# Delta-rule step: where the sums of squares and the turned values stand in the matmul queue

## The reference, cut to what matters

```
mixed_qkv = silu(causal_depthwise_conv(hidden @ Wqkv.T, conv_w))   # 4 taps
query, key, value = split(mixed_qkv)       # z, b, a: further projections of hidden
q = l2norm(query) / sqrt(128);  k = l2norm(key)
per token: state = state * exp(g);  delta = (v - k.state) * beta
           state = state + k (x) delta;  out = q.state
out = rmsnorm(out) * norm_w * silu(z);  result = out @ Wout.T
```

## Time and profile before

| | us |
|---|---|
| three runs | 4674.03, 4670.1, 4676.54 |
| the profiled execution | 4684.11, span 4682.3 |
| `l3_attn`, full steps (first to last copy of cT that is read below) | 2458.5 to 3906.4 |
| busy in the whole span: TensorE matmul, VectorE, ScalarE, GpSimd | 3980.4, 3125.7, 2219.9, 1512.9 |

### The profile page before, as it was taken

One profiled execution on the slowest core, in us unless ns is written; L12 is line 12 of the kernel. 1 busy time (PEld: TensorE's weight loads), 2 busy tenths in 40 slices (PEclk: granted clock), 3 DMA queues, 4 the chain that ended last, 5 costly groups with the idle time before them and its releaser, 6 DMA issues. The chain is left out here.

```text
span 4682.3 us, 143164 instructions
## 1 busy us (share of the span) xinstructions
PE 3980.4 (85%) x62044; PEld 2624.8 (56%) x62052; DVE 3125.7 (67%) x5769; ACT 2219.9 (47%) x4151; POOL 1512.9 (32%) x1605
## 2 busy tenths in 40 slices
PE   7627886677777887999799999999999999689999
PEld 6515654323323665344577777777777776455555
DVE  7897744788887887765577777777777776521111
ACT  3446542654443555322566666666666665221111
POOL 1001200088895221000443444444444443112222
PEclk9858997898998999999899999999999999789999
DMA  1000000133332000100200000000101000041111
GB/s 35 19 27 11 2 13 21 43 114 122 125 130 82 2 2 22 34 1 1 52 22 22 25 22 22 25 22 22 26 22 26 24 13 4 7 135 53 54 50 43
DMA packets 72969, 175.13 MB, mean 37 GB/s; under 512 B 14578, under 2 KB 27892, under 8 KB 69748
## 3 DMA queue, kind: packets, MB, share of 16 engines
q1 hardware_dynamic: 72340, 165.96, 11.3%
HBM read 163.04 MB, written 2.88 MB: 35 GB/s over the span
## 5 line engine op out<-in xcount | busy, mean ns | idle before, releaser
L1721 POOL TENSOR_TENSOR ssm_ub<-ssm_dtu,ssm_bcn 128x512 f32<-128x512 f32 x256 | 324.8, 1295 | 297.2 <-DMA ssm_bcn<-ssm_bct 294.8
L3084 DVE TENSOR_TENSOR moe_hh<-moe_si,moe_pu 128x512 f32<-128x512 f32 x104 | 71.4, 687 | 450.5 <-PE moe_pu L2973 444.3
L2525 POOL TENSOR_TENSOR dn_gm<-dn_cb,dn_cs 128x256 f32<-128x256 f32 x128 | 76.9, 622 | 672.9 <-DMA dn_cb<-dn_cum 438.9
L3017 ACT ACTIVATE moe_si<-moe_pg 128x512 f32<-128x512 f32 x104 | 62.1, 597 | 467.5 <-PE moe_pg L2973 467.5
L1620 ACT ACTIVATE ssm_da<-core_XN,ssm_al 128x504 f32<-128x504 f32 x240 | 163.2, 683 | 253.3 <-DVE ssm_ph L1788 169.0
L2541 POOL TENSOR_TENSOR dn_eb<-dn_ee,dn_cc 128x512 f32<-128x512 f32 x64 | 66.8, 1044 | 652.5 <-DVE dn_cc L2651 652.5
L3036 POOL TENSOR_TENSOR moe_hw<-moe_hh,moe_cb 128x512 f32<-128x512 f32 x100 | 126.8, 1268 | 444.1 <-DVE moe_hh L3084 393.6
L1608 PE MATMUL ssm_py<-ssm_hc,core_ident 128*128 128x512 f32 x352 | 201.4, 678 | 60.8 <-DVE ssm_yy L1773 30.4
L2293 PE MATMUL dn_po<-dn_wo,dn_cT 128*128 128x256 f32 x1024 | 245.1, 394 | 2.3 <-ACT dn_cT L2460 2.2
L2208 PE MATMUL dn_pm<-dn_zz,dn_XB 32*32 32x32 f32 x16384 | 209.2, 195 | 25.3 <-issue 25.2
L1788 DVE TENSOR_TENSOR_SCAN ssm_ph<-ssm_da,ssm_ub 128x512 f32<-128x512 f32 x168 | 205.0, 1220 | 29.3 <-POOL ssm_ub L1721 17.0
(11 more groups left out here) (504 smaller groups left out, 10541.4 us busy)
## 6 DMA issues: line engine op xcount, KB each, us to landing
ssm_bcn<-ssm_bct SPq DMA_DIRECT2D x128, 512.0 KB, 3.7
dn_cb<-dn_cum SPq DMA_DIRECT2D x32, 512.0 KB, 4.8
dn_w<-in_dn_w SPq DMA_DIRECT2D x32, 388.0 KB, 3.5
moe_cb<-moe_rows SPq DMA_DIRECT2D x64, 192.0 KB, 2.8
moe_w<-in_moe_w SPq DMA_DIRECT2D x26, 384.0 KB, 7.1
moe_cb<-moe_rows SPq DMA_DIRECT2D x64, 128.0 KB, 3.0
dn_wo<-in_dn_w SPq DMA_DIRECT2D x16, 256.0 KB, 6.0
moe_cb<-moe_rows SPq DMA_DIRECT2D x64, 64.0 KB, 2.6
```

What stands on the lines that cost most here:

```text
L1721: pool.tensor_tensor(ub[u % NUB][:, :], dtu[q % 2][:, c, :], bcn[i % NB][:, 0, :], ALU.mult).then_inc(ub_ready, 1)
```

## The change

Three pieces of a full step move. Nothing is added or taken away in the arithmetic.

- The sums of squares go from item 8 to between items 4 and 5 and write bB in place of bC. Their waits (`raw_free` twice and `sq_ready`) go with them. ScalarE copies them out right behind the squaring, ahead of its copy of round three.
- The transpose of the sums goes from item 10 to between items 6 and 7, also into bB; VectorE makes `rb` ahead of the key norms. The gate's first half then waits for `tq_done`, its second half for `raw_free`.
- The turned values go in front of `first(i+1)`, and on ScalarE their copies go in front of `tap(i+1, 0)`.

```
--- before.py
+++ after.py
                         mm.then_inc(y_ready, 1)
+                    if new:
+                        take(pe, raw_free, 2)
+                        take(pe, sq_ready)
+                        for j in range(TPC):
+                            mm = pe.matmul(bB[j * 32:(j + 1) * 32, 0:P], g.ones[:, 0:32], sqq[:, j * P:(j + 1) * P], start=True,
+                                           stop=True, tile_position=(0, j * 32))
+                        mm.then_inc(ssq_ready, 1)
...
                         project(i, 3, bA)
-                        take(pe, raw_free)
+                        take(pe, sqr_ready)
+                        pe.transpose(bB[:, P:2 * P], sqr[:, :], g.ident[:, :]).then_inc(sst_ready, 1)
                         take(pe, silu_ready, 2)
...
                         mm.then_inc(g_ready, 1)
-                        take(pe, raw_free, 2)
-                        take(pe, sq_ready)
-                        for j in range(TPC):
-                            mm = pe.matmul(bC[j * 32:(j + 1) * 32, 0:P], g.ones[:, 0:32], sqq[:, j * P:(j + 1) * P], start=True,
-                                           stop=True, tile_position=(0, j * 32))
-                        mm.then_inc(ssq_ready, 1)
...
                     if new:
-                        take(pe, sqr_ready)
-                        pe.transpose(bC[:, P:2 * P], sqr[:, :], g.ident[:, :]).then_inc(sst_ready, 1)
+                        take(pe, tq_done)
                         gate(i, 0, bB)
-                        take(pe, tq_done)
+                        take(pe, raw_free)
                         gate(i, 1, bC)
...
-                    if i + 1 < NSTEP:
-                        take(pe, pt_done)
-                        first(i + 1)
                     if new:
...
                         values(1, bC)
+                    if i + 1 < NSTEP:
+                        take(pe, pt_done)
+                        first(i + 1)
...
                         act.activation(sqq[:, :], cv[:, 1, :], ACT.Square).then_inc(sq_ready, 1)
+                        take(act, ssq_ready)
+                        act.activation(sqr[:, :], bB[:, 0:P], ACT.Copy).then_inc(sqr_ready, 1)
...
                         tap(i, 3, bA)
-                        take(act, ssq_ready)
-                        act.activation(sqr[:, :], bC[:, 0:P], ACT.Copy).then_inc(sqr_ready, 1)
...
+                    if new:
+                        values(i, 0, bA)
+                        values(i, 1, bC)
                     if i + 1 < NSTEP:
                         tap(i + 1, 0, bD)
                     if new:
-                        values(i, 0, bA)
-                        values(i, 1, bC)
                         roots(i)
...
                     if new:
+                        take(dve, sst_ready)
+                        dve.tensor_scalar(rb[i % 4][:, :], bB[:, P:2 * P:32], 1e-6, 128e-6, ALU.add, ALU.mult).then_inc(tq_done, 1)
                         take(dve, g_ready)
...
                     if new:
-                        take(dve, sst_ready)
-                        dve.tensor_scalar(rb[i % 4][:, :], bC[:, P:2 * P:32], 1e-6, 128e-6, ALU.add, ALU.mult).then_inc(tq_done, 1)
                         take(dve, eb_ready)
```

## The result

| us | before | after |
|---|---|---|
| median of four runs each | 4673.4 (4670.1 to 4676.5) | 4738.0 (4731.9 to 4749.9) |
| the profiled execution | 4684.1 | 4731.9 |

The ratio is 1.0134, with a 95% interval of 1.0118 to 1.0149: some 63 us slower. The forecast was 4690, the range 4668 to 4708. `l3_attn`, from its first matmul (at 2231.7 us before, 2227.9 after) to the next sub-block's, takes 51.4 us more in them; it started 3.9 us earlier, for reasons outside the change.

A forecast was written before the change was run, and what follows sets the result against it. TensorE's own work was taken to bound the kernel, 25.71 of 26.81 us a step, the rest mostly gaps awaiting instruction blocks. Terms 17.6 - 3.5 + 2.5 = 16.6 us on the median gave 4690 us, range 4668 to 4708.

The forecast's parts named there:

- The mechanism: TensorE's instruction fetch hangs on the sums' wait for the squaring; its later block lengthens gaps at round three's end.
- A: Gap at the end of round three, 7 of 54 steps before; longer and more frequent after, net +17.6 us.
- More slow clock behind longer gaps: Term for slow-clock stretches following longer TensorE gaps: 0, at most +6 us.
- B: Gap in round four, L2330 or just behind, 21 of 54 steps before; -3.5 us, bounds -14 and +6.
- C: Gap in round one, 12 of 54 steps before; fetch asked for later, +2.5 us, bounds -5 and +6.
- Slower in every step: Rival: sequencer stands at `sq_ready`, round three starts 0.3 us late each time; 4708 us, chance 0.14.
- No change: Rival: margin holds, fetches do not hang on the new wait, gains and losses cancel; 4674 us, chance 0.22.
- faster: Rival: fetch does not hang on the wait, round four's block is asked for earlier; 4663 us, chance 0.14.

The follow-up runs named there:

- e6: Changed kernel, order untouched, but squaring writes two buffers in turn and sums read the previous step's squares, their wait long satisfied; 4687.5 us, ratio 1.0025.
- e5: Kernel before with one more VectorE instruction in each step, ahead of the update that round two waits for; 4704.1 us, ratio 1.0058.
- e4: Changed kernel with the sums behind round three instead of in front of it; 4686.9 us, ratio 1.0020.
- e2: Kernel before with the third piece alone, the turned values in front of first(i+1); 4675.0 us, ratio 0.9997.
- e3: Changed kernel, but steps 0 to 3 keep the old place of the sums, their transpose and their readers; 4727.4 us, ratio 1.0110.
- p4: Changed kernel with 17 round-one matmuls issued twice (1536 records a step), boundary about 18 records behind the output projection's start; 4922.8 us, ratio 1.0512.
- p3: Kernel before with 17 round-one matmuls issued twice (1536 records a step), boundary about 18 records behind the output projection's start; 4790.2 us, ratio 1.0228.
- p1: Kernel before with 17 round-one matmuls issued twice (1536 records a step), boundary 45 records ahead of the output projection; 4852.2 us, ratio 1.0356.

## Why the prediction was wrong

- **The mechanism was right.** The step without gaps stayed at 25.7 us, round three and the gram came 0.37 and 0.47 later, the packet comes 5.6 to 6.6 us after the mark, and most of the gaps are 1.3 to 2.5 us. The forecast said 1.5 to 2 us behind a packet at 5.5 to 5.8. e6 shows that the wait for the squaring does it. What failed are the sizes of three terms of the sum, each too small.
- **The width of A failed.** I took 48 + 8 records, 13 of 60 steps; there were 19 of 59. I had let VectorE's chain come 0.47 later and called it harmless, because no one waits for it. A count by place says where the difference lies. Take the boundary that is passed around the output projection, the one whose crossing lets the block for round three's end be asked for, and count its records from the projection's first. Before the change the packet behind it is late for all boundaries but one at -5 to +29, 9 steps. In the changed kernel it is late for all but one at -25 to +47, 17 steps (and two gaps of A come from +54 and +57). The upper end moved as forecast. The lower end did not stand in the forecast: at -25 to -7 five packets come 5.6 to 5.8 us after the mark, where in the kernel before five at -27 to -11 came at 1.8 to 2.1. The packet ahead of these came 1.6 to 2.8 us before the mark there and 0.5 to 1.2 before it in the changed kernel, so it is late already. My reading is that the sequencer meets VectorE's update in the look-ahead, at the head of round two; its block comes later, and the next one then misses its chance before the sequencer stands at the sums' wait. e5 (late from -27 on in all but one, 15 steps, with TensorE's queue untouched) shows that a later VectorE does this; e6 and e4 (late from -27 and -28, 18 and 19 steps) have the later chain without the long wait; e2, without the later chain, has 11 steps, though it too reaches down to -17. Gaps of A grew by 27.3 us where the sum had 17.6 for all of it.
- **The clock failed.** "More slow clock behind longer gaps: 0, at most +6" was 10 us in the profile. In these 59 steps of the profile before, 4 of 13 gaps of over 1.1 us have half clock behind them, 3.41 us each time. By that share 11 more long gaps would have had 3 or 4 such stretches, +6 us and not 0. The profile after has nine stretches, eight of them in steps whose gap A was 1.77 us or more, of which there are 12.
- **The first steps failed, by 10 us (e3: 10.6).** I priced the wait in a full step, with 0.31 us to spare behind an output projection, and multiplied by 60. The first four steps have no output projection, and the sum had no term for them.
- **B and C came out, in part by luck:** the gaps of B went down by 3.3 us (the sum had 3.5; its own terms, 1.4 x 1.3 and 22 x 0.1, make 4.0), those of C up by 1.8 (2.5). But e2, which is as fast as the kernel before, has 27.8 us in B and 6.6 in C, 1.4 more and 3.1 less than that kernel, so two profiles scatter by more than the agreement. Round two's 2.6 us and round five's 1.3 stood in no term. With steps so late one must tell the gaps by place, not by time: at 2923.15 the gap is in round four, 15.6 us after the mark.
- "Slower in every step" did not happen: the margin held, and the steps without gaps kept their 25.7 us. "No change" and "faster" needed a fetch that does not hang on the new wait, and e6 shows that it does.

The Trainium skill, Advanced Engine Details and Errata, ISA Cache, gives lines of 256 instructions and two of them. The runs agree with the 256: all 55 gaps of the kernel before and all 66 of the changed one in the 59 steps stand at one remainder of the record number by 256, and 1536 records hold them in place. They fit two lines as well, since a late packet is followed by a gap at the very next boundary.

Open: in the medians the change costs 64.6 us, in the two profiles 51.4 in `l3_attn`. Half clock differs between executions that are otherwise alike (13.7 us in the full steps of the profile before, none in those of e2, which is as fast), which may be the rest. The granted clock of the whole execution hints at it: it was 0.932 in the profiled run of the changed kernel and 0.928 in its slowest, 4749.9 us. Where in the kernel that lies the unprofiled runs can't show.

## What to carry over

In this kernel a semaphore wait on TensorE cost more than its own length. While the sequencer stood at it, ahead of the array and unseen among TensorE's waits, the next block of instructions did not come (its packet moved from 4.1 to 5.8 us after the mark with the wait, and back in e6), and behind a dense stretch of small matmuls that came back as an "issue" gap, later and elsewhere. Before moving a wait ahead of dense work, ask when it is satisfied, not only whether the array would wait for it, and price it also in the first and last steps, where its cover is missing. And a later chain on another engine isn't free because no one waits for it, if a wait in the look-ahead hangs on it: 1.00 us more on VectorE in each step cost 0.58%, 27 us, in e5.

## What was not expected of the hardware

- From a packet's start to the restart at the end of round three it took 2.2 to 3.0 us in every variant. In the changed kernel the late packet came 1.2 to 2.2 us behind the squaring's end, in half of the steps within 1.4.
- Behind a gap of 2.21 us the granted clock was 0.50 for 6.83 us, though TensorE had work again after 0.52 us of it. In p4, with gaps of 2.0 and 1.3 us in 58 steps, half clock summed to 139.9 us, against 75 us in p3 with gaps of 0.4 and 1.3 us.
- Two boundaries in 324 records of tiny matmuls gave a gap in each step of p1, 2.0 us on average and up to 2.5: a block of 256 is used up in 1.3 us, and from its packet's start to the restart it took 2.2 and more.
